# The end of a chunked scan on one core: where GpSimd issues its gathers, where VectorE steps the state, and where it splits the first middle slices

## The reference

```python
def step(state, inp):                       # _ssd_scan, per token
    x_t, b_t, c_t, dt_t = inp
    decay = jnp.exp(dt_t * a)[..., None, None]
    b_bar = dt_t[..., None] * b_t
    state = decay * state + b_bar[..., None] * x_t[:, :, None, :]
    y_t = jnp.einsum('bhn,bhnp->bhp', c_t, state)
    return (state, y_t)
...
G_t, idx_t = jax.lax.top_k(Sm.T, k)         # _L0_ffn_ref, 8 experts, k = 1024 tokens each
tokens = xf[idx]
mid = jax.nn.silu(jnp.einsum('keh,ehf->kef', tokens, Wu) + bu)
out = jnp.einsum('kef,efh->keh', mid, W_down) + b_down
y = jnp.zeros_like(xf).at[idx].add(G[..., None] * out)
...
xn = _layernorm(x, axis=-1)
s = _L0_attn_ref(xn, ...)                   # projection, conv, scan, group norm, gate, projection
g = _silu(_L0_ffn_ref(xn, ...))
x = x + s * g
```

## Time and profile before

| what | value |
|---|---|
| median of 3 runs | 1298.08 us (1296.4 to 1298.24) |
| the profiled execution | 1298.12 us, of which its span 1296.3 us |
| PE busy | 1268.6 us (98%), 10327 matmuls |
| DVE, POOL, ACT busy | 952.3 (73%), 770.7 (59%), 627.3 us (48%) |
| chain that ended last | PE 83%, DVE 10%, POOL 3% |
| gathers, L1445 | 64 issues, 67.2 us busy on POOL, mean 1050 ns |

### The profile page before, as it was taken

The page is one execution under the profiler, slowest core; times in us unless marked ns, Lnnn a source line. Parts: engine busy times, 40 slices in busy tenths (PEclk is TensorE's granted clock), DMA queues, the critical chain, the costliest instruction groups (busy, mean ns, idle before and its releaser), DMA issues.

```text
span 1296.3 us, 26583 instructions
## 1 busy us (share of the span) xinstructions
PE 1268.6 (98%) x10327; PEld 1056.3 (81%) x10329; DVE 952.3 (73%) x1936; ACT 627.3 (48%) x1295; POOL 770.7 (59%) x658
## 2 busy tenths in 40 slices
PE   8899999999999999999999998999999999999999
PEld 4566577888888888888888887799899989899998
DVE  7999876777766566676776655798777765787786
ACT  5888885344343433434443333444444332555554
POOL 3777855344444556655766555456666655577774
PEclk9999999999999999999999999899999999999999
DMA  8574355734544444445345444475454545787884
GB/s 280 173 257 172 146 211 165 162 123 131 170 151 145 139 155 130 156 139 179 124 128 172 127 138 149 135 207 110 90 115 91 95 87 119 222 262 253 265 273 150
DMA packets 121435, 210.54 MB, mean 162 GB/s; under 512 B 18400, under 2 KB 91872, under 8 KB 112992
## 3 DMA queue, kind: packets, MB, share of 16 engines
q1 hardware_dynamic: 108160, 191.62, 45.6%
q0 software_dynamic: 12288, 17.05, 7.8%
q10 hardware_dynamic: 864, 0.19, 0.1%
HBM read 140.93 MB, written 67.90 MB: 161 GB/s over the span
## 4 chain that ended last, share of the span: by engine, by line
PE 83%; DVE 10%; POOL 3%; issue 1%; another core or an unknown queue 1%; ACT 1%; DMA 0%; SPq 0%; POOLq 0%; DVEq 0%; ACTq 0%
PE ps L1184 24%; PE ps L1523 10%; PE ps L1780 9%; PE ps L2003 7%; PE ps L1982 7%; PE ps L1239 5%; PE ps L1308 5%; PE ps L1271 3%; PE ps L1320 3%; POOL acc L507 2%; PE ps L1254 2%; DVE acc L263 2%; PE ps L1288 2%; DVE acc L255 2%; PE ps L618 2%; PE ps L1845 1%
## 5 line engine op out<-in xcount | busy, mean ns | idle before, releaser
L1151 ACT ACTIVATE decay<-tap,ncum 128x128 f32<-128x128 f32 x344 | 105.4, 389 | 143.2 <-POOL tap L1064 138.5
L1708 POOL DMA_INDIRECT ffn_dram<-ob,idx x64 | 109.7, 1715 | 82.4 <-DVE ob L1627 68.7
L983 DVE TENSOR_TENSOR yb<-ps,yb 128x256 f32<-128x256 f32 x128 | 48.4, 420 | 126.9 <-PE ps L1320 106.6
L1742 ACT ACTIVATE mid<-ps,b_up 128x512 f32<-128x512 f32 x96 | 66.1, 689 | 154.4 <-PE ps L1523 139.1
L1093 POOL TENSOR_SCALAR yb<-x,dcol 128x512 f32<-128x512 f32 x64 | 45.5, 712 | 155.3 <-DMA y_dram<-yb 92.1
L1070 POOL TENSOR_TENSOR x_lo<-x,x_hi 128x512 fp32r<-128x512 f32 x56 | 74.8, 1335 | 80.7 <-ACT x_hi L1137 80.5
L1081 POOL TENSOR_TENSOR c_dec<-cT,ecum_row 128x512 f32<-128x512 f32 x64 | 87.0, 1360 | 37.7 <-PE ps L1320 26.9
L507 POOL TENSOR_TENSOR acc<-acc,tap 128x512 f32<-128x512 f32 x64 | 82.1, 1286 | 32.7 <-DVE acc L263 31.6
L1184 PE MATMUL ps<-x_hi,w_hi_c 128*128 128x512 f32 x240 | 99.6, 415 | 0.0
L1184 PE MATMUL ps<-x_hi,w_hi_b 128*128 128x512 f32 x240 | 99.5, 415 | 0.1
L1865 POOL TENSOR_SCALAR yc<-yc,gn_scale,gn_shift 128x512 f32<-128x512 f32 x56 | 87.4, 1572 | 16.4 <-DMA yc<-y_dram 16.3
(11 more groups left out here) (308 smaller groups left out, 4073.9 us busy)
## 6 DMA issues: line engine op xcount, KB each, us to landing
tap<-cum_dram SPq DMA_DIRECT2D x43, 512.0 KB, 5.4
x_dram<-x SPq DMA_DIRECT2D x16, 1024.0 KB, 5.3
x<-x_dram SPq DMA_DIRECT2D x16, 1024.0 KB, 5.9
ecum_row<-ecum_dram SPq DMA_DIRECT2D x128, 128.0 KB, 3.1
y_dram<-yb SPq DMA_DIRECT2D x16, 1024.0 KB
yc<-y_dram SPq DMA_DIRECT2D x16, 1024.0 KB, 5.9
cum_row<-cum_dram SPq DMA_DIRECT2D x21, 512.0 KB
rows_dram<-xn SPq DMA_DIRECT2D x16, 512.0 KB, 3.0
```

What stands on the lines that cost most here:

```text
L1151: n = nc.scalar.activation(decay[g % 2][:, h, :], cum_row[g % NR][:, h, :], ACT.Exp, bias=t.ncum[:, g, h:h + 1])
L1708: pool.indirect_dma_start(out=t.ffn_dram, out_offset=bass.IndirectOffsetOnAxis(ap=t.idx[:, e, h * HC + c:h * HC + c + 1], axis=0), in_=ob[ ...
```

## The change

Four edits. (1) `update` is called with the chunk's own number behind its output addition L983, in place of the step for the chunk before behind `mix`. This holds in all 64 chunks. (2) On POOL the expert parts stand directly behind `decay_c(g)`, ahead of the low parts, `scale_x` and the list values. (3) The gathers of the third pass go from chunk 61 to chunk 63. (4) DVE splits slices 0 and 1 in chunk 63 (before: 0 and 1 in chunk 62, 2 in chunk 63), and slice 2 in the experts' phase, where `DONE` is 2 in place of 3.

```diff
@@ chunk(g), DVE
                                 decay[g % 2][:, 4 * i:4 * i + 4, :], ALU.mult).then_inc(mix_ready, 1)
-            if g:
-                update(g - 1)
             if LIST0 - 1 <= g < LIST1 - 1:
                 list_slots(g - LIST0 + 1)
...
             if LAST <= g < LAST + 2:
                 x.token_lo(dve, c)
-            elif g >= LAST:
-                for f in ((0, 1), (2,))[c - 2]:
+            elif g == NT - 1:
+                for f in range(2):
                     x.middle(dve, 0, f)
             dve.wait_ge(y_mm, g + 1)
...
             n.then_inc(y_ready, 1)
+            update(g)
@@ the chunks' loop, POOL
             decay_c(g)
+            if LAST - 2 <= g < LAST:
+                x.gather(pool, *x.passes[g - LAST + 2])
+            elif g == LAST:
+                x.split_up_lo(pool, nc.gpsimd, 0)
+            elif g == NT - 1:
+                x.gather(pool, *x.passes[2])
             if b + 2 < NB:
                 lo_part(b + 2, c)
             if b + 1 < NB:
                 scale_x(b + 1, c)
             if LIST0 - 1 <= g < LIST1 - 1:
                 list_values(g - LIST0 + 1)
-            if LAST - 2 <= g < LAST:
-                x.gather(pool, *x.passes[g - LAST + 2])
-            elif g == LAST:
-                x.split_up_lo(pool, nc.gpsimd, 0)
-            elif g == LAST + 1:
-                x.gather(pool, *x.passes[2])
@@ phase_experts
-    FIRST, DONE = 5, 3
+    FIRST, DONE = 5, 2
```

## The result

The changed kernel takes **1291.18 us** (median of 6 runs, 1290.77 to 1291.93) where the kernel before took 1298.16 beside it (6 runs, 1296.03 to 1299.89). The ratio is 0.9948, with a 95% interval of 0.9935 to 0.9961: 7.0 us less, where 6.3 were forecast (1291.8, range 1287.5 to 1295.5). The profiled execution took 1290.77 us with a span of 1288.9.

What follows compares the result with a forecast made beforehand. PE was busy 98% of the span, so only its idle and low-clock time, 11.5 us near the scan's end, could be won. 8.9 - 1.6 (tail) - 1.0 (clock) = 6.3 us off 1298.12 gave 1291.8 us, range 1287.5 to 1295.5.

Steps and rivals of the forecast that it cites:

- Both holds of chunks 58 and 59 go: Chunks 58 and 59: with gathers behind `c_dec`, PE's output signals arrive late no more; chunk 58's had come 4.2 us late.
- the rival that the hold covers every signal: Chunk 59: the transposes' signal also waits for the last gather, L1288 stands 3.5 us; 1295.3 us, chance 0.15.
- The state's step costs 0.5 us in chunk 58 and nothing in ordinary chunks: Step behind the output: 2.0 us of cover hides it in ordinary chunks; in chunk 58 PE loses 0.5 us.
- L931 waits for the POOL operation that it meets: State's step on DVE: L931 waits for POOL's current operation and ends 0.3 us behind it, beside `c_dec` or `split_up_lo`.
- The milestones: Starts of PE's output blocks (L1308), chunks 58 to 63, forecast one by one from 791.7 to 829.5 us.
- A new collision in chunk 63, L981 1.3 us late: Chunk 63: the third gathers lie over the output block, so the output add (L983 before the change) starts 1.3 us late.
- the 0.4 that I took: Chunk 63: two DVE casts beside the gathers lengthen them by 0 to 0.84 us; the middle, 0.4, was taken.
- The tail's cost, 1.6 us, as a wait in `down`: Experts' phase: slice 2's split 1.07 plus late L983 1.3 less cover 0.8 gives 1.6 us of PE wait for L1626.
- The clock, 1.0 us: Chunks 60 and 61: PE still idles about 1.2 and 0.9 us; its clock may fall, costing 0 to 2, taken 1.0.
- the 11.5 us: Last five chunks of the scan: PE's loss to waits and low clock, 1.4 plus 10.1 us, the change's ceiling.
- 8.9: Up to chunk 63's output block: us won, its start moving from 838.45 to 829.5.
- while POOL issues gathers over an output block: Scan: PE's semaphores reach others only after the last gather; three of three groups there, none of 13 in the experts' phase.

## Why the prediction was right, point by point

- **Both holds of chunks 58 and 59 go.** Right. No "remote" wait of L981 is left, and the two groups alone are worth 5.3 us. But the change did not put to the test the rival that the hold covers every signal: in chunk 59 the transposes of x ended at 795.89, and the first gather started at 795.90. That was luck, as the prediction had that gather start 0.3 us ahead of the signal.
- **The state's step costs 0.5 us in chunk 58 and nothing in ordinary chunks.** Right: chunk 58 took 10.09 us in place of 9.73, 0.36 lost, and an ordinary chunk 9.73 (792.06 to 801.79). That it takes 0.8 us out of chunk 60's way was no gain: alone it gave none, and without it the end of the scan was 0.47 us shorter. It won 0.34 us in chunk 60 and lost 0.55 in chunk 61, where L931 stands behind `up_lo`.
- **L931 waits for the POOL operation that it meets.** Right: 1.09 beside `c_dec`, 1.36 beside `up_lo`, and it ended 0.3 us behind each. The rule of the Trainium skill ("SBUF — State Buffer", "Who interferes with whom") held here.
- **The milestones.** Counted from chunk 57's block they were forecast at 10.2, 19.9, 26.4, 34.1, 41.4 and 48.1 us and came at 10.1, 19.8, 26.2, 33.5, 40.6 and 47.1. The error, 0.9 us, is in chunks 60 to 63: `x_dt` of chunk 61 came earlier behind `up_lo` (L931 ended 30.5 us behind chunk 57's block, not 31.0), and a short chunk takes PE 7.07 and 6.53 us, not 7.3 and 6.7.
- **A new collision in chunk 63, L981 1.3 us late.** 1.4 in the trace. The two casts beside the gathers lengthened the last one to 1.04 from 0.95, 0.1 us in all, not the 0.4 that I took, nor the 0.84 by the rule of the Trainium skill ("SBUF — State Buffer", "SBUF: two separate sides"). The rest of the lateness is the hold itself, 0.9 us and not 0.8.
- **The tail's cost, 1.6 us, as a wait in `down`.** The size was near (1.83), the place only in part. The wait for L1626 gave 1.07; 0.76 came as a wait of `up` for ACT's `mid`. The prediction looked at ACT's slices 3 and 4 and not at slice 5, which waits for the split of slice 2, and that split stands behind the late L981. Putting the slices back won 1.1 us by the medians and 1.02 in the tail.
- **The clock, 1.0 us.** The mis-sized term: 0. PE idled 1.02 us in front of chunk 60's block and 0.66 in chunk 61 at a granted clock of 1.00. The reading under it was wrong too: PE did not idle 3.2 us before its clock fell, for L1288 already took 1.11 us against 0.60, and it stands ahead of the wait of 0.92. And the low clock had come twice, with 0.67 and 0.84.
- **What was lost before.** The waits for `x_dt` and the state and one low clock are part of the 11.5 us. The prediction's account leaves out PE's two stops in the scores of chunk 61, 1.89 us, and the low clock behind them.

In sum 9.86 - 1.83 = 8.0 us against 8.9 - 1.6 - 1.0 = 6.3; some 0.6 us less are seen in the spans, of which 0.5 lie ahead of chunk 57, where the start of that chunk scatters over 1.4 us. So the total lies nearer to the forecast than its terms do: 1.0 us too little up to block 63 and 1.0 too much for the clock miss in the same direction, and 0.2 in the tail and the scatter took part of it back.

**What stays open** is the mechanism of the hold. The prediction took it as a pattern ("while POOL issues gathers over an output block"), and for this change that was enough. As a rule it is wrong at both ends: other signals were held too (the transposes of b, under the last gather of a group, and in the kernel before the scores and the transposes of x), and on the third chip nothing was. Nor is the experts' phase free of it, as the prediction held: in the kernel before a signal of `down` (L1782), due at 905.06 under an indirect DMA of L1708, came 1.46 us late, and DVE's L1627 started only at 906.55. No wait of PE came of it. On the third chip the kernel before was as slow all the same (1297.14 us, its granted clock over the span 0.996 to 0.998 as on the other chips), and moving the gathers won as much there. But no trace of it was taken on that chip, so whether its late arrivals were there, or what else it lost, is not shown.

## What to carry to other kernels

A wait that ends "remote", on an engine whose partner has finished by its own records, is worth following to what a third engine was doing then. Here it led to GpSimd's gathers, and moving GpSimd's work alone was worth as much as the whole change or more (0.9938 against 0.9948, with intervals that overlap). Test each part of a compound change by itself: the place of the work on GpSimd made the gain, the state's step cost half a microsecond in the traces, and the slices cost one. And before work is put on an engine "with slack", look at what it stands for in its idle time: GpSimd, busy 6 of 10 us, could not take 5 us more in one chunk of four without stopping TensorE.

## What the runs showed of the hardware that was not expected

- The output block's signal came 1.4 to 4.3 us late where it fell under a group of GpSimd's gathers, in all but one case 0.8 to 1.2 us behind the last gather, on two chips; on a third, 0.04 us, with the same instructions at the same distance. In the kernel before the signals sent behind a held one came within 0.3 us behind it; some others under gathers were on time on the same chips.
- In chunk 61 with gathers over its block, TensorE itself stood 0.78 and 0.94 us in the scores with nothing to wait for, and its granted clock was 0.83 over the ten us behind; in the kernel before it was 0.95 and 0.94 us and 0.84. Each time the second stop ended within 0.1 us of the arrival of L1254's held signal (820.49 and 820.54; 825.48 and 825.56), which is a pattern and no cause.
- Eight plain copies on GpSimd's queue took 4.28 us to issue, four gathers 4.8: a DMA of 128 rows costs GpSimd 0.54 us as a copy and 1.26 as a gather.
